# Expert rows written to their token's place inside the expert loop, and loaded plainly in the final stage

## The reference

```python
x = x + tanh(g_xattn) * cross_attention(layernorm(x), ctx)
x = x + tanh(g_ffn) * moe(layernorm(x))

def moe(x2):                       # x2: 2048 x 512
    shared_out = (silu(g_s) * u_s) @ shared_w_down.T   # inner width 512
    probs = softmax(x2 @ gate_w.T)                     # 16 experts
    topk_vals, topk_idx = top_k(probs, 2)              # weights divided by their sum
    out_e = (silu(g) * u) @ w_down.T                   # per expert, inner width 128
    return sum of each token's two out_e, weighted, + shared_out
```

## Time and profile before

| | |
|---|---|
| median of 3 runs | 1465.6 us (1465.59 to 1466.02) |
| the profiled execution's own time | 1465.77 us |
| its span in the profile | 1464.0 us |
| expert loop, first to last down product | about 1250 to 1396 us |
| final stage | about 1397 to 1464 us |

### The profile page before, as it was taken

One profiled execution on the slowest core, in us unless ns is written; L12 is line 12 of the kernel. 1 busy time (PEld: TensorE's weight loads), 2 busy tenths in 40 slices (PEclk: granted clock), 3 DMA queues, 4 the chain that ended last, 5 costly groups with the idle time before them and its releaser, 6 DMA issues.

```text
span 1464.0 us, 27092 instructions
## 1 busy us (share of the span) xinstructions
PE 1419.2 (97%) x9085; PEld 1128.1 (77%) x9086; DVE 847.3 (58%) x1816; ACT 501.0 (34%) x1097; POOL 317.9 (22%) x330
## 2 busy tenths in 40 slices
PE   6999997999999999999999999999999999999995
PEld 5888876787777877778787777877777888777773
DVE  5444446565666656666565666656687653344375
ACT  4333343333333333333333333333334421222220
POOL 1222223212122121211212121121212101232462
PEclk9999999999999999999999999999999999999997
DMA  6544440111111111111101111111122343655565
GB/s 225 164 122 136 122 118 30 47 30 40 37 40 40 30 47 37 34 36 40 41 29 49 37 33 39 38 40 33 59 71 81 126 170 138 230 164 170 153 195 171
DMA packets 91097, 125.95 MB, mean 86 GB/s; under 512 B 7376, under 2 KB 56528, under 8 KB 90512
## 3 DMA queue, kind: packets, MB, share of 16 engines
q1 hardware_dynamic: 84704, 104.16, 22.5%
q0 software_dynamic: 6320, 20.71, 5.1%
HBM read 87.36 MB, written 37.49 MB: 85 GB/s over the span
## 4 chain that ended last, share of the span: by engine, by line
PE 91%; issue 3%; DVE 2%; DMA 2%; POOL 1%; ACT 1%; SPq 0%; POOLq 0%; DVEq 0%; ACTq 0%
PE ps L549 23%; PE ps L551 22%; PE ps L550 22%; PE ps L879 5%; PE ps L615 4%; PE ps L657 4%; PE ps L895 3%; PE ps L623 2%; PE ps L642 2%; PE ps L874 1%; PE ps L596 1%; DMA acc<-in_wv 1%; DMA wgu<-in_w_gu 1%; DVE acc L1660 1%; PE ps L793 1%
## 5 line engine op out<-in xcount | busy, mean ns | idle before, releaser
L1046 ACT CAST ah<-ps 128x256 fp32r<-128x256 f32 x256 | 83.4, 382 | 238.5 <-PE ps L551 234.6
L470 POOL CAST vth<-vt 128x256 fp32r<-128x256 f32 x64 | 25.7, 402 | 637.6 <-PE ps L657 637.6
L1284 DVE TENSOR_TENSOR acc<-ps,acc 128x512 f32 (+1 forms) x129 | 88.6, 687 | 129.9 <-PE ps L551 129.9
L549 PE MATMUL ps<-hT,w0h 128*128 128x512 f32 (+1 forms) x384 | 153.9, 401 | 0.9 <-DVE w0l L1232 0.9
L551 PE MATMUL ps<-hT,w0h 128*128 128x512 f32 (+1 forms) x384 | 150.6, 392 | 0.0
L550 PE MATMUL ps<-hT,w0l 128*128 128x512 f32 (+1 forms) x384 | 150.0, 391 | 0.0
L464 POOL TENSOR_TENSOR qr<-qv,mhalf 128x8 f32<-128x8 f32 x64 | 105.6, 1649 | 90.0 <-DVE qv L1299 90.0
L1290 DVE TENSOR_TENSOR al<-ps,ah 128x256 fp32r<-128x256 f32 x256 | 95.7, 416 | 50.6 <-ACT ah L1046 50.6
L1013 ACT COPY qs<-ps 128x512 f32<-128x512 f32 x128 | 75.2, 587 | 134.9 <-PE ps L551 131.4
L1022 ACT ACTIVATE pb<-pb 128x256 f32<-128x256 f32 x128 | 48.2, 418 | 175.3 <-DVE pb L1315 175.3
L549 PE MATMUL ps<-w1l,ah 128*128 128x512 f32 x260 | 105.3, 405 | 1.0 <-DVE al L1290 1.0
(11 more groups left out here) (223 smaller groups left out, 3033.8 us busy)
## 6 DMA issues: line engine op xcount, KB each, us to landing
wraw<-in_w_att SPq DMA_DIRECT2D x64, 256.0 KB, 2.6
ybuf<-ye SPq DMA_DIRECT2D x47, 256.0 KB, 2.0
vbuf<-vo SPq DMA_DIRECT2D x16, 512.0 KB, 3.3
kbuf<-ko SPq DMA_DIRECT2D x16, 512.0 KB, 3.8
kt<-kbuf SPq DMA_DIRECT2D x32, 256.0 KB, 2.9
vt<-vbuf SPq DMA_DIRECT2D x64, 128.0 KB, 2.0
wgu<-in_w_gu SPq DMA_DIRECT2D x4, 2048.0 KB, 9.3
craw<-in_ctxT SPq DMA_DIRECT2D x9, 512.0 KB, 4.9
```

What stands on the lines that cost most here:

```text
L549: pe.matmul(dst, l_hi, r_lo, start=first, stop=False)
L1046: act.copy(ah[:, bp, :, b2, :], pv_view(bp, b2)).then_inc(a_hi, 1)
L1284: dve.tensor_tensor(dst, PS[6 + bp][:], dst, ALU.add).then_inc(acc_done, 1)
```

## The change

- `ybuf` now has two halves of 2048 rows, one for the first and one for the second expert of each token, and 256 spare rows for padding. The slot table carries token + 1, and 2048 more for the second expert, so that DVE can make two lists from it: `sidx` (the token to gather) and `didx` (the row of `ybuf` to write; padded slots get a spare row).
- The store of block b moves from SP (a plain DMA) to POOL (an indirect DMA, `scatter`), where it stands behind the gather of block b+6.
- The split of the down weights is cut into 8 pieces and put between POOL's gathers, at every fourth block from 16 to 44.
- In the final stage the 32 gathers on POOL are gone. SP loads, for each token tile, both rows of all 128 tokens with one plain DMA of 512 KB (`load_y`), 8 tiles ahead.
- The first row is weighted by ACT (one instruction a tile, in place) and added to `acc` by POOL (one a tile). DVE keeps the second row's weighted addition. DVE does all of `act_rest` first, and then `combine` and `shared_out` in groups of 4, 4 and 8 tiles.

```diff
-    y_t = ybuf.rearrange("(n p) d -> n p d", p=P)
+    y_t = ybuf[0:2 * T].rearrange("(s n p) d -> n p s d", s=2, p=P)
...
-            def store_block(b, q):
-                sp.wait_ge(ye_ok, b + 3)
-                sp.dma_start(y_t[b], ye[q][:]).then_inc(y_st[q], 16)
...
+            def load_y(n):
+                if n >= YT:
+                    sp.wait_ge(add2, n - YT + 1)
+                sp.dma_start(y[n % YT][:], y_t[n]).then_inc(y_in[n % YT], 16)
+
+            def store_out(n):
+                sp.wait_ge(sh_done, n + 1)
                 sp.dma_start(out[n], acc[:, n, :]).then_inc(out_st, 16)
+
+            sp.wait_ge(y_st[0], 16 * (NB // 2) + 16)
+            sp.wait_ge(y_st[1], 16 * (NB // 2))
+            for n in range(YT):
+                load_y(n)
+            for z in range(2):
+                for n in range(4 * z, 4 * z + 4):
+                    load_y(YT + n)
+                for n in range(4 * z, 4 * z + 4):
+                    store_out(n)
+            for n in range(8, NT):
+                store_out(n)
...
+            def scatter(b):
+                pool.wait_ge(ye_ok, b + 3)
+                pool.indirect_dma_start(ybuf, bass.IndirectOffsetOnAxis(didx[:, b:b + 1], 0),
+                                        ye[b % 2][:], None).then_inc(y_st[b % 2], 16)
+
+            def split_down(z):
+                cs = slice(256 * z, 256 * z + 256)
...
+            for b in range(6):
+                gather(b)
+            pool.wait_ge(didx_ok, 1)
+            for b in range(6, NB):
+                gather(b)
+                scatter(b - 6)
+                if b >= 16 and b % 4 == 0 and b < 48:
+                    split_down(b // 4 - 4)
+            for b in range(NB - 6, NB):
+                scatter(b)
+
             for n in range(NT):
-                if n >= YT:
-                    pool.wait_ge(add2, n - YT + 1)
-                for s in range(2):
-                    pool.indirect_dma_start(y[s][n % YT][:], None, ybuf,
-                                            bass.IndirectOffsetOnAxis(sli[:, s, n:n + 1], 0)).then_inc(y_in[s][n % YT], 16)
+                pool.wait_ge(y_scaled, n + 1)
+                pool.tensor_tensor(acc[:, n, :], y[n % YT][:, 0, :], acc[:, n, :], ALU.add).then_inc(add1, 1)
...
+            for n in range(NT):
+                act.wait_ge(y_in[n % YT], 16 * (n // YT) + 16)
+                act.activation(y[n % YT][:, 0, :], y[n % YT][:, 0, :], ACT.Copy, scale=cw[:, 0, n:n + 1]).then_inc(
+                    y_scaled, 1)
...
+            for c in range(4):
+                act_rest(c)
+            for n0 in (0, 4):
+                for n in range(n0, n0 + 4):
+                    combine(n)
+                for n in range(n0, n0 + 4):
+                    shared_out(n)
+            for n in range(8, 16):
                 combine(n)
-                shared_out(n, after_combine=True)
+            for n in range(8, 16):
+                shared_out(n)
```

More of the change, by code:

```diff
@@ L67, in build @@
     h2buf = nc.dram_tensor("h2buf", [T, D], F32, kind="Internal").ap()
-    ybuf = nc.dram_tensor("ybuf", [NB * P, D], F32, kind="Internal").ap()
+    ybuf = nc.dram_tensor("ybuf", [2 * T + 2 * P, D], F32, kind="Internal").ap()
     k_pair = kbuf.rearrange("(d c) p n -> d p c n", c=2)
@@ L98, in build @@
         sidf = sb("sidf", [P, 2 * NB])
+        didx = sb("didx", [P, NB], I32)
+        spare = sb("spare", [P, NB + 1])
         acc = sb("acc", [P, NT, D])
@@ L178, in build @@
         with ExitStack() as a:
-            y = [[sb(f"y{s}{q}", [P, D], F32, a) for q in range(YT)] for s in range(2)]
+            y = [sb(f"y{q}", [P, 2, D], F32, a) for q in range(YT)]
         wdn = sb("wdn", [P, E, D])
@@ L261, in build @@
         y_in, add1, add2, out_st = (
-            [[sem(f"y{s}_in{q}") for q in range(YT)] for s in range(2)], sem("add1"), sem("add2"), sem("out_st"))
+            [sem(f"y_in{q}") for q in range(YT)], sem("add1"), sem("add2"), sem("out_st"))
+        y_scaled = sem("y_scaled")
         dve_mark, pool_mark = sem("dve_mark"), sem("pool_mark")
@@ L285, in _ @@
         def _(sp):
-            for s in (v_stored, k_stored, *y_st, *h2_stored, wgu_last):
+            for s in (v_stored, k_stored, *h2_stored, wgu_last):
                 sp.sem_inc(s, 16)
@@ L503, in _, with gather @@
                 pool.wait_ge(h2_stored[q], 16 * (NT // 4) + 16)
-            for b in range(NB):
+            def gather(b):
                 if b >= 3:
@@ L943, in _ @@
             expert_down(NB - 1, 0)
-            pe.wait_ge(shd_lo, 1)
+            pe.wait_ge(shd_lo, 8)
             down_by_slice(0)
@@ L1616, in _ @@
             link(dve.tensor_copy(sidf[:], PS[7][:, 0:2 * NB]))
-            dve.tensor_tensor(sidx[:], sidf[:, 0:NB], sidf[:, NB:2 * NB], ALU.add).then_inc(sidx_ok, 1)
+            placed, spared = sidf[:, 0:NB], sidf[:, NB:2 * NB]
+            link(dve.tensor_tensor(placed, placed, spared, ALU.add))
+            link(dve.tensor_scalar(didx[:], placed, -1.0, 0.0, ALU.add, ALU.max))
+            dve.tensor_scalar(sidx[:], didx[:], T - 1, None, ALU.bitwise_and).then_inc(sidx_ok, 1)
+            link(dve.scalar_tensor_tensor(out=spared, in0=placed, scalar=0.0, in1=spare[:, 0:NB], op0=ALU.is_equal,
+                                          op1=ALU.mult))
+            dve.wait_ge(sidx_ok, 1)
+            dve.scalar_tensor_tensor(out=didx[:], in0=placed, scalar=-1.0, in1=spared, op0=ALU.add,
+                                     op1=ALU.add).then_inc(didx_ok, 1)
             for it in range(4):
@@ L1626, in _, with dve_block @@
             gated(0, 0)
-            def dve_block(b, q):
+            def dve_block(b, q, first=False):
                 dve.wait_ge(eT_done, b + 1)
@@ L1633, in dve_block @@
                 dve.wait_ge(ed_done, b + 1)
-                dve.wait_ge(y_st[q], 8 * (b - q) + 16)
+                if not first:
+                    dve.wait_ge(y_st[q], 8 * (b - q))
                 dve.tensor_copy(ye[q][:], PS[5 + q][:]).then_inc(ye_ok, 1)
-            with dve.Fori(0, PAIRS) as m:
+            for b in range(2):
+                dve_block(b, b, first=True)
+            with dve.Fori(1, PAIRS) as m:
                 for q in range(2):
@@ L1650, in act_rest, with combine, shared_out @@
                                       act_hl[:, c, it, 0, :], ALU.subtract).then_inc(act_lo, 1)
[L1652 to L1666, removed]
+            def combine(n):
+                dve.wait_ge(add1, n + 1)
+                dve.scalar_tensor_tensor(out=acc[:, n, :], in0=y[n % YT][:, 1, :], scalar=cw[:, 1, n:n + 1],
+                                         in1=acc[:, n, :], op0=ALU.mult, op1=ALU.add).then_inc(add2, 1)
+            def shared_out(n):
+                dve.wait_ge(add2, n + 1)
                 dve.wait_ge(dn_done, n + 1)
```

54 lines of the change are left out of this document (12 added, 42 removed).

## The result

The changed kernel takes **1447.62 us** (median of 4 runs, 1445.57 to 1447.74) against 1465.81 us of the kernel before on the same chip (4 runs, 1465.59 to 1466.86). The ratio is 0.987 with a 95% interval of [0.9854, 0.9886]. The profiled execution took 1447.74 us with a span of 1445.7.

A forecast was written before the change was run, and what follows sets the result against it. PE was taken to bound the kernel, with a final-stage gap from dense indirect DMAs. -17.75 - 1.4 = -19.15 us against 1465.77 gives 1446.6, set to 1446.5 us because the profiled execution lay 0.17 over the median; range 1444 to 1460.

The forecast's parts named there:

- The gap: Final stage, 1427 to 1445: PE idles under dense indirect DMAs; replacing the gathers by plain loads saves 17.75 us.
- The tail: End of final stage: DVE's last addition starts about 0.5 us after the last matmul, not 1.88; saves 1.4 us.
- PE's five feeders: Final stage: load start, load traffic, ACT and POOL work, DVE work and free banks all keep up, so PE sets the end.
- The rival of excluding additions: Final stage: POOL's and DVE's additions only alternate, 16 pairs taking 32.5 us; 1449.5 us in all; chance 0.07.
- The store on POOL and the split in 8 pieces: Expert loop: scatters and split pieces on POOL fit under the slack and cost nothing.
- The slack of 1.6 us: Expert loop: scatter lands 0.9 us before DVE wants `ye` again, plus 0.72 us that DVE idles.
- the first rival: Expert loop: denser indirect DMAs slow blocks until their spacing is tolerable; 19 us at 1.78, 57 at 2.2; chance 0.07.
- The earlier start: Loop's start: weight loads gain a little because stores come later; sets the range's lower end, 1444 us.
- Traffic of any kind: Final stage: plain loads bring the gap back in part or whole, 1448 to 1464 us; chance 0.10, half for the whole.
- POOL as the bound of the loop: Expert loop: both DMAs at 1.46 + 0.30 make blocks 3.52 us, costing 17 us; 1464 to 1474 us; chance 0.05.

The follow-up runs named there:

- e2: Kernel before, the final stage's 32 gathers replaced by 32 plain 256 KB loads from SP of as many rows: 1449.26 us.
- e4: Kernel before, 32 gathers of as many rows but 512 bytes of each instead of 2048: 1469.58 us.
- e1: Kernel before, POOL's program ending only when the last tile is stored: 1476.43 us, against 1467.82 before on the same chip.
- e5: Kernel before, the 16 gathers of the second rows replaced by plain loads from SP, the first rows' 16 still indirect on POOL: 1451.18 us.
- e3: Kernel before, a small POOL copy of 128 columns behind each of the final stage's 32 gathers: 1461.54 us.
- e10: Changed kernel with both additions on DVE, plus 32 unused POOL gathers of 512 bytes a row with eight landing places in the final stage: 1460.44 us.
- e11: The changed kernel as it is, timed again on another occasion: 1451.84 us, ratio 0.9902 to the kernel before.
- e8: Changed kernel with both additions on DVE, plus 32 unused POOL gathers with three landing places in the final stage: 1472.98 us.
- e6: Changed kernel, the 8 pieces of the split moved out of the loop's steady part, behind the last 6 scatters: 1449.12 us, ratio 0.9877.

## Why the prediction was right

The forecast was 1446.5 us in 1444 to 1460; 1447.62 was measured. Between the two profiled executions the difference is 1465.77 - 1447.74 = 18.03 us, where the sum said 19.15.

- **The gap goes, -17.75.** Right. PE's 191 steps take 43.41 us, and the cause that the prediction only inferred from times is now shown: not traffic (e2), not the gathers' bytes (e4), not POOL's ending (e1), but a long run (e5) of indirect DMAs that follow each other closely (e3 parts them by a copy). The prediction read their spacing as 1.25 us throughout. That holds only from 1430 on; up to 1426.59, just before PE stalls, 20 steps are 1.37 us in the mean. The forecast didn't rest on it. The prediction also said that no row shows how. e10 gives one step of it: what PE signals arrives late, by up to 15 us. The rest of the mechanism is open.
- **The tail, -1.4.** Right: the last addition starts 0.49 us after the last product, against 0.5.
- **PE's five feeders.** The loads start at 1401.05 (1400.9 said), ACT's last row is there at 1430.26 (1431 said), ACT takes 0.72 us (0.70 said). POOL's addition is 1.28 us at its shortest, as estimated. What the forecast had wrong is that it stays so beside DVE. The rival of excluding additions holds in its mechanism. Its price was too high: it charged 2.03 us for a pair, and a pair takes 1.71. It was to cost 3 us and cost nothing, because DVE is done with all tiles but the last at 1440.51, 1.97 us before it can have the last.
- **The store on POOL and the split in 8 pieces, nothing.** This is the step that failed, by 1.45 us, 0.70 of it idle time (3.23 and 1.92 us in e11). The durations were right: 0.97 to 1.00 us for a scatter where 0.95 was taken, and 1.2 us for a piece against at most 1.7. The slack of 1.6 us was counted for the buffer, though, and DVE never waited for a scatter's landing. The time went by the way of the first rival, the gap that moves into the loop: the pieces push gathers and scatters together to 1.3 us for four in a row, and PE's signals come late. That rival's price was for a loop that slows down as a whole until its spacing is tolerable; measured is about half a microsecond for each of three waits in 47 blocks.
- **The rest.** With 1.45 us lost in the loop and a start 0.57 us earlier the final stage begins 0.89 us later, and the time outside the span is 2.04 us, not 1.77. Together that is 1.16 us, and the sum missed by 1.12. The earlier start, of which the prediction's range spoke, is luck as far as the runs show: the same place varies by 3.5 us among e1 to e3. Without it the sum would have missed by 1.7. The second measurement of the same kernel, e11's 1451.84, lies 5.3 us over the forecast and still in the range.
- **Traffic of any kind** is refuted by e2. **POOL as the bound of the loop** too: a gather beside the loop's DVE copies takes 0.97 us. But the lock-out on which that rival rested exists in the final stage, where a gather of 0.95 us took 6.63 beside DVE's splits (e8).

## What to carry to other kernels

Idle time of PE that the profile puts down to "issue" is to be laid beside the other engines' timelines before it is taken for PE's own: here it was POOL's run of indirect DMAs, and plain loads of as many rows, or even a useless copy between the gathers, freed PE. Where rows are both written and read by index, the side that has the slack for it should do the indexing, and its indirect DMAs should be spread, since a bunch of four already delays signals. An addition moved from DVE to POOL saves DVE next to nothing while DVE's own instructions read two SBUF inputs; it should be timed beside them, not alone.

## What the runs showed of the hardware

- **A dense run of indirect DMAs delays what TensorE signals and then TensorE itself.** PE was held for good after 15 of them at 1.29 us in the mean (e4) and 21 at 1.37 (the kernel before). It was not held after 21 at 1.42 (e10), nor by 32 at 1.73 with a copy between them (e3). Where the limit lies between these, and whether spacing alone sets it, is open. Plain loads at 358 GB/s don't do it (e2). Why the dense run does is open too. Each time here is that of a recorded execution, and whether PE is held in one that isn't recorded was not tried. The Trainium skill (NOTIFIC — the notification-queue block, Overflow: three behaviours, one of which stalls the engine) says that the block which writes the records holds its producers back when its inner queues are full, rather than lose a record. That would fit an engine that stalls without waiting for anything, but no run here shows it. What the traces do show is that records are missing there: from 1420 to 1445, 18 instructions of the kernel before raise a semaphore and 7 such records exist, while e2 has all 46. So an idle time put down to "issue" beside indirect DMAs can also be a wait whose record is lost.
- **POOL's program ends late.** With a wait for the last store at its end, the span went on for 9.05 us after DVE's last addition in place of 2.5, with a DRAIN of 6.53 us on POOL (e1). In e8, where POOL ends last, the DRAIN took 5.50 us. This is hidden as long as POOL is done early.
- **A gather issued while DVE subtracts from SBUF to SBUF can be locked out**: 6.63 us in e8 and 6.47 in e10, where 0.95 is usual, until 0.85 us after DVE's last split. The scatter before it took 1.17 us beside the same splits. The Trainium skill (SBUF — State Buffer, Who interferes with whom) holds that such a DVE instruction takes only the read side from GpSimd, and infers that the making of descriptors is not concerned; the two measured gathers speak against that inference, and the scatter doesn't.
- **POOL arithmetic and DVE's splits slow each other**: 16 splits took 18.98 us beside POOL's pieces and additions, and 9.71 without (e6).
